# All transpose-bank evictions on VectorE, and the next head's expansion moved ahead of the last iteration's matmuls, in an eight-core latent-attention kernel

## The chip, the cores and the metric

The kernel runs on the eight cores of one Trainium2 chip. Its time is device microseconds of the slowest core, from a run of the whole program. Each core computes the same steps on its own rows of the input; there is no exchange between cores.

## The reference

One layer of latent attention and a gated low-rank feed-forward part, each followed by a residual and a layer norm. Batch 2, sequence 4096, model width 4096, 32 heads. Cut to what matters:

```python
q   = _rmsnorm(x @ wq_a.T, q_a_ln_w) @ wq_b.T            # 32 heads x 128
ckv, k_pe = split(x @ wkv_a.T)                           # 256 latent + 64 rope
kv  = _rmsnorm(ckv, kv_a_ln_w) @ wkv_b.T                 # per head: 64 k_nope + 128 v
# rope on q_pe and k_pe, k_pe shared by all heads
scores = einsum('bqhd,bkhd->bhqk', q_full, k_full) * softmax_scale
attn   = softmax(where(causal, scores, min))
out    = einsum('bhqk,bkhd->bqhd', attn, v) @ wo.T
x = _layernorm(x + out)
# feed-forward: 64 experts of rank 8, top 16 gated by a small router
x = _layernorm(x + ((x @ A_w.T) * gate) @ B_w.T * 2.0)
```

## The kernel before

A core owns 1024 of the 8192 query rows: eight tiles of 128, spread so that each core has the same causal work. The stages run one after the other with a barrier between them: the latent keys of all 4096 positions; the query's first and second projection; the attention loop over 32 heads; the output projection with layer norm; the router; the feed-forward part and the last layer norm. Activations lie transposed on chip.

Every instruction is recorded by the helper class `Em` and replayed by `_replay`, whose line 267 emits them all. So each row of the profile says L267, and instructions are told apart by their tiles. Orders and waits are written out by hand: `em.op(engine, ...)` appends to an engine's queue, `em.mark(engine)` gives a token, `em.wait(engine, token)` makes that engine's queue stop until the token is there. Each engine runs its queue strictly in the order in which `em` recorded it.

The attention loop stands in lines 799 to 890. An iteration is one head, one slot (a tile of 128 queries; eight slots, `NSLOT`) and one block of 1024 keys. Slots need 1, 2, 3, 4, 1, 2, 3, 4 blocks (`TRIPS`, line 27), so a head has 20 iterations and the loop has 640. Iteration `r` of the loop records, in this order:

- ScalarE: the exponential of the scores of `r`, from bank `sA` or `sB` (by the parity of r) into `P_sb`. It waits for QK of `r` and the transposes of `r-2`.
- TensorE: QK of `r+1` (two matmuls of 512 columns into the other score bank), which needs the exponential of `r-1` to have left that bank.
- TensorE: PV of `r-1` (eight matmuls into `mix` or `mix2`), which waits for the eviction of `r-1`.
- TensorE: eight transposes of `P_sb` into `ptP`, which wait for the exponential of `r`. Their token is `tok_pvt[r]`.
- If `r-1` was the last block of its slot, the finish of that slot: VectorE reciprocal and multiply, a TensorE transpose into `mix`, a VectorE copy into the output tile (`fin_done`, `fin_act_prev`).
- The eviction of `ptP` into `PT_sb`, token `tok_evac[r]`: with the causal mask on VectorE if `r` is the last block of its slot; otherwise a plain copy, on VectorE for even `r` and on ScalarE for odd `r` (line 870).

Keys and values of a head are made from the latent ones by `emit_expansion` (line 740), just before the head's first iteration: eight blocks, each with 2 matmuls for the keys, which VectorE casts into `Kf`, and 8 matmuls for the values, which ScalarE casts into `Vx`. All of it goes through one score bank, and each block's key matmuls wait for the cast of the block before, and likewise the value matmuls. `Kf` and `Vx` have two buffers. At a head boundary, that is where `nxt["h"] != cur["h"]`, the QK of the next iteration is not recorded in its usual place: the expansion and that QK stand at the end of the iteration (lines 882 to 886), behind PV, the transposes and the eviction.

Of the kernel before, what the change touches and what calls it, by code (L numbers as in the profile page):

```python
# [294 lines left out]
def build(debug=False, race_detect=True, upto="F"):  # L295
# [56 lines left out]
    with ExitStack() as ctx:  # L352
        em = Em(nc, ctx)
        _LAST_EM[0] = em
        _emit(nc, em, d, ctx, debug, upto)
        _replay(nc, em, ctx)
# [3 lines left out]
def _emit(nc, em, d, ctx, debug, upto="F"):  # L360
# [332 lines left out]
    with ExitStack() as pctx:  # L693
# [9 lines left out]
        scores = [sA, sB]  # L703
# [17 lines left out]
        for h in range(H):  # L721
            for s in range(NSLOT):
                for kb in range(TRIPS[s]):
                    if s == 0 and kb == 0:
                        first_it[h] = len(iters)
                    iters.append(dict(h=h, s=s, kb=kb, first=(kb == 0),
                                      last=(kb == TRIPS[s] - 1)))
# [3 lines left out]
        tok_exp = [None] * N  # L731
# [8 lines left out]
        def emit_expansion(h, bank):  # L740
            hp = h % 2
            war = tok_flash_done.get(h - 2)
            ev = []
            kn_ev = [None] * 8
            v_ev = [None] * 8
            em.waits("pe", [t_wkvb])
            for b in range(8):
                if b >= 1:
                    em.wait("pe", kn_ev[b - 1])
                for c in range(2):  # L750
                    em.opw("pe", [t_wkvb], "matmul", bank[0:64, 0:512],
                           wkvb_sb[c][:, h * 192: h * 192 + 64],
                           cnorm[c][:, b * 512:(b + 1) * 512],
                           start=(c == 0), stop=(c == 1))
                t_kn = em.mark("pe")
                em.waits("dve", [t_kn, war, t_init, t_init_p])
                em.op("dve", "tensor_copy", Kf[hp][0:64, b * 512:(b + 1) * 512],
                      bank[0:64, 0:512])
                kn_ev[b] = em.mark("dve")
                ev.append(kn_ev[b])  # L760
                if b >= 1:
                    em.wait("pe", v_ev[b - 1])
                for sub in range(4):
                    kk = b * 4 + sub
                    for c in range(2):
                        em.opw("pe", [t_wkvb], "matmul",
                               bank[:, 512 + sub * 128: 512 + sub * 128 + 128],
                               cnorm[c][:, kk * 128:(kk + 1) * 128],
                               wkvb_sb[c][:, h * 192 + 64: h * 192 + 192],
                               start=(c == 0), stop=(c == 1))  # L770
                t_v = em.mark("pe")
                em.waits("act", [t_v, war, t_init, t_init_p])
                dst = Vx[hp][:, b * 4 * VSTRIDE:(b + 1) * 4 * VSTRIDE]
                dst = dst.rearrange("p (s w) -> p s w", w=VSTRIDE)[:, :, 0:128]
                em.op("act", "copy", dst,
                      bank[:, 512:1024].rearrange("p (s w) -> p s w", w=128))
                v_ev[b] = em.mark("act")
                ev.append(v_ev[b])
            tok_exp_ready[h] = ev

        def emit_qk(it):
            cu = iters[it]
            par = it % 2
            hp = cu["h"] % 2
            if it - 2 >= 0:
                em.wait("pe", tok_exp[it - 2])
            em.waits("pe", tok_exp_ready.get(cu["h"], []))
            kb = cu["kb"]
            lhsQ = Q[:, cu["h"] * 1024 + cu["s"] * 128: cu["h"] * 1024 + cu["s"] * 128 + 128]
            for hh in range(2):  # L790
                em.op("pe", "matmul", scores[par][:, hh * 512:(hh + 1) * 512],
                      lhsQ, Kf[hp][:, kb * 1024 + hh * 512: kb * 1024 + hh * 512 + 512],
                      start=True, stop=True)
            tok_qk[it] = em.mark("pe")
# [4 lines left out]
        for r in range(N + 1):  # L799
            prev = iters[r - 1] if r >= 1 else None  # L800
            cur = iters[r] if r < N else None
            nxt = iters[r + 1] if r + 1 < N else None

            if cur is not None:
                par = r % 2
                em.wait("act", tok_qk[r])
                if r - 2 >= 0:
                    em.wait("act", tok_pvt[r - 2])
                em.op("act", "activation", P_sb[par][:], scores[par][:], AF.Exp,
                      scale=SCALE)  # L810
                tok_exp[r] = em.mark("act")

            boundary = (nxt is not None and cur is not None
                        and nxt["h"] != cur["h"])
            if nxt is not None and not boundary:
                emit_qk(r + 1)

            if prev is not None:
                parp = (r - 1) % 2
                sp = prev["s"] % 2  # L820
                em.wait("pe", tok_evac[r - 1])
                if prev["first"] and fin_done[sp] is not None:
                    em.wait("pe", fin_done[sp])
                em.waits("pe", [fin_act_prev[0]])
                hpp = prev["h"] % 2
                kbp = prev["kb"]
                for t in range(8):
                    em.opw("pe", [tok_evac[r - 1]], "matmul", pv_[sp],
                           PT_sb[parp][:, t * 128:(t + 1) * 128],
                           Vx[hpp][:, (kbp * 8 + t) * VSTRIDE:  # L830
                                     (kbp * 8 + t) * VSTRIDE + 129],
                           start=(prev["first"] and t == 0),
                           stop=(prev["last"] and t == 7))

            if cur is not None:
                em.wait("pe", tok_exp[r])
                if r - 2 >= 0:
                    em.wait("pe", tok_evac[r - 2])
                for t in range(8):
                    em.opw("pe", [tok_exp[r]], "transpose",  # L840
                           ptP[par][:, t * 128:(t + 1) * 128],
                           P_sb[par][:, t * 128:(t + 1) * 128], idn16[:])
            tok_pvt[r] = em.mark("pe")

            if prev is not None and prev["last"]:
                sp = prev["s"] % 2
                h_, sf = prev["h"], prev["s"]
                em.wait("dve", tok_pvt[r])
                if fin_pe_prev[0] is not None:
                    em.wait("dve", fin_pe_prev[0])  # L850
                em.op("dve", "reciprocal", rcp_c, pv_[sp][:, 128:129])
                em.self_edge("dve")
                em.op("dve", "tensor_tensor", att_tm, pv_[sp][:, 0:128],
                      rcp_c.broadcast_to((128, 128)), op=ALU.mult)
                t_fin = em.mark("dve")
                fin_done[sp] = t_fin
                em.waits("pe", [t_fin, fin_act_prev[0]])
                em.opw("pe", [t_fin], "transpose", atp, att_tm, idn16[:])
                t_atp = em.mark("pe")
                fin_pe_prev[0] = t_atp  # L860
                em.wait("dve", t_atp)
                em.op("dve", "tensor_copy",
                      Q[:, h_ * 1024 + sf * 128: h_ * 1024 + sf * 128 + 128],
                      atp)
                fin_act_prev[0] = em.mark("dve")
                if sf == NSLOT - 1:
                    tok_flash_done[h_] = fin_act_prev[0]

            if cur is not None:
                e = "dve" if (cur["last"] or r % 2 == 0) else "act"  # L870
                em.wait(e, tok_pvt[r])
                if cur["last"]:
                    fam = 0 if cur["s"] < 4 else 1
                    em.op(e, "tensor_tensor", PT_sb[par][:], ptP[par][:],
                          mask2[:, fam * 1024:(fam + 1) * 1024], op=ALU.mult)
                elif e == "act":
                    em.op(e, "copy", PT_sb[par][:], ptP[par][:])
                else:
                    em.op(e, "tensor_copy", PT_sb[par][:], ptP[par][:])
                tok_evac[r] = em.mark(e)  # L880

            if boundary:
                if r - 1 >= 0:
                    em.wait("pe", tok_exp[r - 1])
                emit_expansion(nxt["h"], scores[(r + 1) % 2])
                emit_qk(r + 1)

        em.barrier()
        if debug:
# [408 lines left out]
```

How the kernel before makes its waits and increments, by code:

```python
        def body(h):  # L264
            for entry in em.stream[e]:
                meth, args, kw, sem, n = entry[:5]
                ins = getattr(h, meth)(*args, **kw)
                for s, v in (entry[5] if len(entry) > 5 else ()):
                    ins._wait_ge(s, v)
                if sem is not None:
                    ins.then_inc(sem, n)
```

## Time and profile before

| | us |
|---|---|
| time, median of 3 runs | 4692.8 |
| time, lowest and highest | 4672.8 and 4705.76 |
| the profiled execution | 4672.8 |
| its span on the slowest core (core 5) | 4671.3 |
| spans of all eight cores | 4646.4 to 4671.3 |
| TensorE busy, share of the span | 2900.7, 62% |
| ScalarE busy | 1229.8, 26% |
| VectorE busy | 1019.7, 22% |
| GpSimd busy | 355.2, 8% |

In rows of the order of time, the columns are start (us from the span's start), duration (us), engine, line, operation, output<-input, shape, count; a bracket gives the idle time of the engine just before and what ended it. PE is TensorE, PEld its weight loads, DVE VectorE, ACT ScalarE; "PEq" and the like are an engine's sequencer, from which a semaphore came, and "issue" is idle time for which the profile shows no wait. A row "x8" is eight instructions back to back, with their total.

### The profile page before, as it was taken

The numbers are of one execution on the slowest core, as the hardware profiler recorded it, in microseconds if no ns is written. First come the engines' busy times: TensorE is split into PE (matmuls) and PEld (weight loads), VectorE is DVE, ScalarE is ACT, GpSimd is POOL, SyncE is SP. The second block draws the span as 40 slices with busy tenths as digits, with TensorE's granted clock in tenths as the row PEclk, the third lists the DMA queues.
The fourth block names the chain that finished last, engine by engine and source line by source line (L and its number), as shares of the span: only waits on it lengthen the run. The fifth ranks groups of instructions, "written<-read, shape, count | busy, mean of one in ns | idle before, by whom it ended". The sixth has DMA issues, their size and how long they took to land.

```text
span 4671.3 us, 53309 instructions; the slowest of 8 cores (4646.4 to 4671.3 us)
## 1 busy us (share of the span) xinstructions
PE 2900.7 (62%) x19214; PEld 1416.4 (30%) x19214; DVE 1019.7 (22%) x1923; ACT 1229.8 (26%) x1280; POOL 355.2 (8%) x466
## 2 busy tenths in 40 slices
PE   2771734444666666666676666666668888827650
PEld 0220311111333334333344333333333333302110
DVE  0110000001222222222222222222220000062116
ACT  0000001111444444444444444444430000000110
POOL 4431002322000000000000000000010000000000
PEclk9886977776989999999978999999999999957775
DMA  8867140002000000000000000000033333210003
GB/s 120 117 90 121 24 72 0 0 0 45 1 1 1 1 1 1 1 1 1 1 1 1 1 1 1 1 1 1 1 57 85 81 82 82 67 37 0 0 0 144
DMA packets 76490, 145.64 MB, mean 31 GB/s; under 512 B 12306, under 2 KB 53396, under 8 KB 70228
## 3 DMA queue, kind: packets, MB, share of 16 engines
q0 software_dynamic: 67792, 116.29, 14.9%
q1 hardware_dynamic: 8452, 25.95, 1.5%
q8 instruction: 169, 2.77, 0.2%
q14 instruction: 77, 0.63, 0.0%
HBM read 233.31 MB, written 16.78 MB: 54 GB/s over the span
## 4 chain that ended last, share of the span: by engine, by line
PEldq 32%; issue 18%; PEld 16%; DVE 14%; ACT 7%; DMA 4%; POOL 2%; DVEq 2%; POOLq 2%; ACTq 1%; another core or an unknown queue 1%; SPq 0%
PEldq L267 32%; DVE AR L267 14%; ACT AR L267 7%; PEld mix L267 4%; PEld psE L267 3%; PEld sA L267 3%; POOL AR L267 2%; DVEq L267 2%; POOLq L267 2%; PEld psL L267 1%; ACTq L267 1%; PEld ptP L267 1%; DMA AR<-xT 1%; DMA AR<-wqbT 1%
## 5 line engine op out<-in xcount | busy, mean ns | idle before, releaser
L267 PE MATMUL sA<-AR 128*128 128x128 bf16 (+2 forms) x3200 | 546.5, 296 | 186.7 <-issue 55.9
L267 PE MATMUL mix<-AR 128*128 128x129 bf16 x5120 | 425.2, 229 | 276.5 <-DVEq L267 189.5
L267 PEld LDWEIGHTS mix<-AR 128*128 128x128 bf16 x5120 | 323.0, 101 | 588.4 <-DVEq L267 387.3
L267 PE MATMUL psE<-AR 128*128 128x512 bf16 x2048 | 479.7, 398 | 14.9 <-issue 10.5
L267 PE MATMUL ptP<-idn,AR 128*128 128x128 bf16 x5120 | 422.2, 230 | 37.5 <-ACTq L267 37.5
L267 ACT ACTIVATE AR<-sB,consts 128x1024 bf16<-128x1024 f32 x320 | 356.3, 1113 | 128.4 <-PEq L267 95.9
L267 ACT ACTIVATE AR<-sA,consts 128x1024 bf16<-128x1024 f32 x320 | 356.2, 1113 | 89.4 <-PEq L267 69.2
L267 ACT COPY AR<-ptP 128x1024 bf16<-128x1024 bf16 x192 | 194.3, 1012 | 648.2 <-PEq L267 648.2
L267 PEld LDWEIGHTS ptP<-idn,AR 128*128 128x128 bf16 x5120 | 340.1, 103 | 52.3 <-ACTq L267 48.3
L267 ACT ACTIVATE AR<-AR 128x1024 bf16<-128x1024 bf16 (+3 forms) x76 | 76.4, 1006 | 1042.9 <-DVEq L267 1042.9
L267 PEld LDWEIGHTS sA<-AR 128*128 128x128 bf16 (+1 forms) x3200 | 205.6, 104 | 417.3 <-issue 394.4
L267 PEld LDWEIGHTS psE<-AR 128*128 128x128 bf16 x2048 | 205.6, 101 | 289.8 <-issue 74.2
L267 ACT CAST AR<-sA 128x512 bf16<-128x512 f32 x256 | 149.8, 585 | 417.7 <-PEq L267 408.8
L267 DVE TENSOR_TENSOR AR<-ptP,AR 128x1024 bf16<-128x1024 bf16 x256 | 177.1, 692 | 361.3 <-PEq L267 353.3
L267 PE MATMUL psL<-AR 128*128 128x512 bf16 (+1 forms) x768 | 186.2, 408 | 89.7 <-DMA AR<-xT 82.8
L267 DVE CAST AR<-sA 64x512 bf16<-64x512 f32 x256 | 174.8, 683 | 273.8 <-PEq L267 272.0
L267 PE MATMUL sB<-AR 128*128 128x512 bf16 x640 | 208.3, 410 | 25.7
L267 DVE COPY AR<-ptP 128x1024 bf16<-128x1024 bf16 x192 | 132.8, 692 | 418.6 <-PEq L267 410.8
L267 PE MATMUL psC<-AR 128*128 128x512 bf16 x512 | 176.0, 520 | 65.5 <-DMA AR<-wqbT 58.6
L267 PE MATMUL mix<-idn,AR 128*128 128x128 bf16 x256 | 56.3, 220 | 246.5 <-DVEq L267 246.5
L267 POOL DMA_DIRECT2D AR<-A_sta x32 | 16.9, 664 | 2317.3 <-DVEq L267 2317.3
L267 PE MATMUL psB<-AR 128*128 128x512 bf16 x512 | 114.5, 386 | 103.2 <-DMA AR<-wqaT 103.2
(91 smaller groups left out, 1734.1 us busy)
## 6 DMA issues: line engine op xcount, KB each, us to landing
AR<-xT POOLq DMA_DIRECT2D x256, 128.0 KB, 9.6
AR<-wo_sta POOLq DMA_DIRECT2D x32, 1024.0 KB, 9.6
AR<-xoT SPq DMA_DIRECT2D x32, 512.0 KB, 9.1
AR<-xoT POOLq DMA_DIRECT2D x32, 256.0 KB, 20.2
AR<-wqaT POOLq DMA_DIRECT2D x4, 2048.0 KB, 65.6
AR<-wqbT POOLq DMA_DIRECT2D x8, 1024.0 KB, 28.0
out<-AR SPq DMA_DIRECT2D x16, 512.0 KB, 2.7
out<-AR POOLq DMA_DIRECT2D x16, 512.0 KB, 2.9
```

What stands on the lines that cost most here:

```text
L267: ins = getattr(h, meth)(*args, **kw)
```

## The change

Two edits in the attention loop. First, the expansion of the next head and the QK of its first iteration no longer stand at the end of the last iteration of a head, but in QK's usual place: ahead of PV of the iteration before and of the last iteration's own transposes. The wait of TensorE for the exponential that frees the score bank moves with them. Second, the eviction of `ptP` is always on VectorE.

```diff
@@ -810,9 +810,11 @@
                       scale=SCALE)
                 tok_exp[r] = em.mark("act")
 
-            boundary = (nxt is not None and cur is not None
-                        and nxt["h"] != cur["h"])
-            if nxt is not None and not boundary:
+            if nxt is not None:
+                if cur is not None and nxt["h"] != cur["h"]:
+                    if r - 1 >= 0:
+                        em.wait("pe", tok_exp[r - 1])
+                    emit_expansion(nxt["h"], scores[(r + 1) % 2])
                 emit_qk(r + 1)
 
             if prev is not None:
@@ -867,7 +869,7 @@
                     tok_flash_done[h_] = fin_act_prev[0]
 
             if cur is not None:
-                e = "dve" if (cur["last"] or r % 2 == 0) else "act"
+                e = "dve"
                 em.wait(e, tok_pvt[r])
                 if cur["last"]:
                     fam = 0 if cur["s"] < 4 else 1
@@ -878,12 +880,6 @@
                 else:
                     em.op(e, "tensor_copy", PT_sb[par][:], ptP[par][:])
                 tok_evac[r] = em.mark(e)
-
-            if boundary:
-                if r - 1 >= 0:
-                    em.wait("pe", tok_exp[r - 1])
-                emit_expansion(nxt["h"], scores[(r + 1) % 2])
-                emit_qk(r + 1)
 
         em.barrier()
         if debug:
```

## Rows read from the trace of the kernel before

**Rows 1.** Spans and mean granted TensorE clock of the cores: the slowest.
```profile
core 5: 4671.3 us, clock 0.858
```

**Rows 2.** The attention loop's stretch: busy us (instructions) per engine, clock, DMA share, GB/s.
```profile
1154.00:3470.00 2316.00, 1563.25 (x14319) 906.38 (x14316) 658.78 (x1470) 1055.98 (x1087) 1.50 (x3) 0.93 0.01 2
```

**Rows 3.** Order of time, one head: T9, its eviction, T10.
```profile
2132.04 0.61 PE L267 MATMUL ptP<-idn,AR 128*128 128x128 bf16 x8
2132.78 0.69 DVE L267 TENSOR_TENSOR AR<-ptP,AR 128x1024 bf16<-128x1024 bf16 x1 [1.37 <-PEq L267]
...
2134.11 0.61 PE L267 MATMUL ptP<-idn,AR 128*128 128x128 bf16 x8
```

**Rows 4.** The same, from T10 to T11: VectorE evicts behind a finish.
```profile
2136.35 0.69 DVE L267 TENSOR_TENSOR AR<-ptP,AR 128x1024 bf16<-128x1024 bf16 x1
...
2137.22 0.62 PE L267 MATMUL mix<-AR 128*128 128x129 bf16 x8 [0.65 <-DVEq L267]
2137.68 0.61 PE L267 MATMUL ptP<-idn,AR 128*128 128x128 bf16 x8
```

**Rows 5.** The same, from T11 to T12: ScalarE evicts beside a finish.
```profile
2138.40 1.01 ACT L267 COPY AR<-ptP 128x1024 bf16<-128x1024 bf16 x1 [3.83 <-PEq L267]
...
2140.47 0.62 PE L267 MATMUL mix<-AR 128*128 128x129 bf16 x8 [0.34 <-issue]
2140.93 0.61 PE L267 MATMUL ptP<-idn,AR 128*128 128x128 bf16 x8
```

**Rows 6.** The same, from T17 to T18: ScalarE evicts, nothing is finished.
```profile
2153.95 0.61 PE L267 MATMUL ptP<-idn,AR 128*128 128x128 bf16 x8
...
2154.67 1.01 ACT L267 COPY AR<-ptP 128x1024 bf16<-128x1024 bf16 x1 [3.83 <-PEq L267]
2155.78 1.11 ACT L267 ACTIVATE AR<-sA,consts 128x1024 bf16<-128x1024 f32 x1
...
2157.06 0.61 PE L267 MATMUL ptP<-idn,AR 128*128 128x128 bf16 x8 [0.59 <-ACTq L267]
```

**Rows 7.** Costliest groups: the plain evictions; busy us, mean ns, idle before and releaser.
```profile
L267 ACT COPY AR<-ptP 128x1024 bf16<-128x1024 bf16 x192 | 194.3, 1012 | 648.2 <-PEq L267 648.2
...
L267 DVE COPY AR<-ptP 128x1024 bf16<-128x1024 bf16 x192 | 132.8, 692 | 418.6 <-PEq L267 410.8
```

**Rows 8.** Order of time at a head boundary: T18, PV, T19, QK, PV, T0.
```profile
2016.64 0.61 PE L267 MATMUL ptP<-idn,AR 128*128 128x128 bf16 x8 [0.59 <-ACTq L267]
...
2018.24 0.62 PE L267 MATMUL mix<-AR 128*128 128x129 bf16 x8 [0.99 <-DVEq L267]
...
2018.70 0.61 PE L267 MATMUL ptP<-idn,AR 128*128 128x128 bf16 x8
...
2033.49 0.59 PE L267 MATMUL sA<-AR 128*128 128x512 bf16 x2 [0.86 <-ACTq L267]
...
2034.85 0.63 PE L267 MATMUL mix<-AR 128*128 128x129 bf16 x8
2035.48 0.61 PE L267 MATMUL ptP<-idn,AR 128*128 128x128 bf16 x8
```

**Rows 9.** Slow transposes: first and last stretched T2 of the 27 heads, one T19.
```profile
1399.96 1.06 PE L267 MATMUL ptP<-idn,AR 128*128 128x128 bf16 x8
...
3276.74 1.06 PE L267 MATMUL ptP<-idn,AR 128*128 128x128 bf16 x8
...
2159.28 1.06 PE L267 MATMUL ptP<-idn,AR 128*128 128x128 bf16 x8
```

**Rows 10.** Stretches of one head each, 27 in a row: first, best, worst, sum and mean.
```profile
1368.40:1448.20 79.80, 56.81 (x450) 32.00 (x451) 20.67 (x47) 33.02 (x34) 0.00 (x0) 0.78 0.00 1
...
2091.50:2161.60 70.10, 46.17 (x449) 26.76 (x447) 20.64 (x46) 33.02 (x34) 0.00 (x0) 0.98 0.00 1
...
2375.60:2458.70 83.10, 60.67 (x450) 34.34 (x451) 20.67 (x47) 33.02 (x34) 0.00 (x0) 0.73 0.00 1
...
sum 1956.00, PE 1324.78 PEld 769.16 DVE 556.99 ACT 891.48 POOL 0.00; mean PE 49.07 PEld 28.49 DVE 20.63 ACT 33.02 POOL 0.00
```

## The prediction, made before the changed kernel was run

> **What bounds the kernel now.** I read the span of the slowest core first. It is 4671.3 us [rows 1], and the profiled execution took 4672.8, so 1.5 us lie around the span. Its time is the lowest of three: the median is 4692.8. Every difference below is worked out in the profiled execution, then taken off the median.
>
> Then I cut the span by stage. The attention loop is the stretch from 1154 to 3470, 2316 us [rows 2]. TensorE is busy 1563 us of it, ScalarE 1056, VectorE 659: nobody is full, so the loop goes by a chain of hand-overs, and busy shares cannot price the change. The change touches nothing outside this stretch.
>
> So I read the order of time inside one head and measured from the start of one transpose group to the next. I call the group of iteration i of a head T0 to T19, and the step to it by the two numbers. There are four kinds of step, and apart from the clock (below) they repeat to 0.02 us:
>
> - *VectorE evicts, nothing else.* T9 at 2132.04, its eviction of 0.69 us at 2132.78, T10 at 2134.11: 2.07 us [rows 3].
> - *VectorE evicts and a slot is finished in between.* The eviction starts only at 2136.35, behind reciprocal, multiply and copy, and PV waits for it ("0.65 <-DVEq"): T10 to T11 is 3.57 us [rows 3, 4].
> - *ScalarE evicts, a slot is finished.* The copy of 1.01 us runs beside VectorE's finish. PV is released by none of the two: T11 to T12 is 3.25 us [rows 4, 5].
> - *ScalarE evicts, nothing finished.* The copy of 1.01 us starts at 2154.67 and the exponential queued behind it at 2155.78. T18 waits for that exponential ("0.59 <-ACTq"), and comes 3.11 us after T17 [rows 6].
>
> **The evictions, one by one.** A head has 20 iterations. Its 8 last ones of a slot are evicted by VectorE anyway, with the mask. Of the other 12, the 6 with odd r go to ScalarE today: iterations 1, 3, 11, 13 (each finishing the slot before) and 7, 17 (plain). That gives 6 x 32 = 192, which is the count of the ScalarE copies [rows 7]. ScalarE's queue loses 192 x 1.012 = 194 us, VectorE's gains 192 x 0.692 = 133 [rows 7]. Neither figure is the gain, since both lie under other work. The price is the kind of step that each becomes:
>
> - 4 x 32 steps go from 3.25 to 3.57: +0.32 each, **+41.0 us**. This is a loss: the eviction, today beside the finish, is queued behind it.
> - 2 x 32 steps go from 3.11 to 2.06: -1.05 each, **-67.2 us**. What is late next there is PV's usual wait for VectorE, which is inside the 2.06.
>
> No other queue moves: ScalarE's exponential no longer has a copy ahead of it, and VectorE at 659 + 133 = 792 us of 2316 is 34% busy.
>
> The Trainium skill speaks against this half of the change: "Use both ScalarE and VectorE for PSUM evacuation" (TensorEngine Tiling (Array Packing), section PSUM Bottleneck). By that rule alone the sum would stop at the first item, a loss; the trace agrees with it on the 128 steps with a finish and not on the 64 without.
>
> **The head boundary.** Today iteration 19's PV waits 0.99 us for the eviction of 18, with no QK to fill the time; then come T19, the expansion of the next head (16 groups into one score bank), two QK, PV, T0. T18 is at 2016.64, T19 at 2018.70, the first QK at 2033.49, T0 at 2035.48: 18.84 us from T18 to T0 [rows 8]. In the new order the expansion stands right behind T18. It needs only the exponential of 18, which T18 already waited for, and the expansion's first VectorE cast stands behind one eviction, as today. So:
>
> - T18 to the first QK: 14.79 us, what T19 to the first QK takes today (2033.49 - 2018.70).
> - first QK, then PV of 18 and T19, both free to run. Today two QK groups take 1.36 us up to PV at 2034.85, 0.68 each, and PV takes 0.63 up to T0 [rows 8]: 0.68 + 0.63 = 1.31 us.
> - T19 to T0: a plain VectorE step with QK inside, 2.06 us.
>
> That makes 18.16, or -0.68 at each of 31 boundaries: **-21 us**. The wait of 0.99 is hidden by the expansion, and the wait for the masked eviction of 19, which the expansion hides today, comes out, but with a QK inside. The finish of slot 7 stays behind T0. The bounds: if QK's place fills nothing, the gain is 0; if the whole 0.99 goes, -31 us. I take -21, by the steps above.
>
> Sum of the hand-overs: 41.0 - 67.2 - 21 = **-47 us**.
>
> **The clock.** The granted clock changes between its two levels, 1.2 and 2.4 GHz, and the rows show it twice over: the whole loop's mean is 0.93 [rows 2], and eight transposes that take 0.61 us take 1.06 [rows 9]. Undisturbed, the steps of a head add up to 68.8 us: 9 steps of 2.06, 4 of 3.57, 4 of 3.25, 2 of 3.11, and 16.78 from T19 to T0 [rows 3 to 6, 8]. The 27 heads from 1368 to 3324 take 72.4 on the mean, 70.1 at best (clock 0.98) and 83.1 at worst (0.73) [rows 10]. So the low clock costs some 3.65 us a head, over twice what the hand-overs of a head promise. I went through all 27 for where it stands:
>
> - T1 to T2 is stretched in 23 of 27, T2 to T3 with it, by 0.8 each on the mean (first and last such T2 [rows 9]): 1.4 us a head. It comes after two thin steps, T0 to T1 (3.57) and the one after.
> - T11 to T12 in 10 of 27, T12 to T13 with it: 0.4 us a head.
> - T19 and the first blocks of the expansion in 19 of 27, after T17 to T18 (3.11, ScalarE's copy) and the 0.99 wait: T19 takes 1.06 [rows 9]. With the expansion's own slow blocks this is about 1.1 to 1.3 us a head, and both worst heads, 79.8 and 83.1 [rows 10], begin with an expansion slow from end to end.
>
> The change takes away both thin places ahead of the third (3.11 becomes 2.06, the bare wait goes): -1.2. It makes four steps thinner (3.57 for 3.25), two of them second in a pair. For T11 to T13 I move the frequency half way to that of T1 (10 to 16.5 of 27, at 1.2): +0.3. T1 to T3 become certain: +0.2. Two single thin steps, priced as T6 to T7 and its follower behave now (0.15 a head): +0.15. Net -0.6 x 32 = **-19 us**; its ends are +48 (1.5 a head more) and -72 (2.25 a head fewer).
>
> Sum: -47 - 19 = -66, or 4607 for an execution like the profiled one, and 4692.8 - 66 = **4627** against the median.
>
> The Trainium skill names the danger: where TensorE idles briefly between groups that cycle through PSUM, its clock gate falls and rises again (TensorE: Matmul & The Clock Gate, A second HAM failure mode). Steps of 3.57 us with a low clock behind them agree with this, and by that rule alone the four thinner steps would cost more than I give them.
>
> **The rivals.**
>
> 1. *The clock gives the gain back* (0.21). The low clock moves with the phase of the heads and falls into every pair of thin steps, and into singles, while the head end stays slow. For it: T1 to T2 in 23 of 27. Against: T16 to T17, a single thin step, is followed by a stretched step in one of 27. -47 + 48: 4693, no change.
> 2. *The clock mostly recovers* (0.17). Without the slow head end, one fall a head is left, costing 1.4: -47 - 72: 4574.
> 3. *Slower: a low clock that holds* (0.08). One mechanism: a fall after T0 to T2 that lasts as in the head at 2375.6, 83.1 us against the mean of 72.4, +10.7 a head [rows 10]. Seven such heads eat the 66 us, eleven make the kernel over 1% slower; fourteen give 4627 + 150 = 4777. Against: both such heads begin at the head end, which gets denser.
> 4. *The freed ScalarE shortens nothing* (0.04). If the plain steps stay at 3.11, because something other than the copy holds them: +41 - 21 = 4713. T9 to T10 at 2.07 speaks against it.
>
> **How the numbers follow.** My forecast has 0.50, alone from 4600 to 4665. A measurement of this kernel tells about 1% from no change, 47 us, so the border is 4646. Faster: 0.17 of rival 2 and 0.42 of my 0.50, 0.59. Slower by over 1%: 0.08. The same: the rest, 0.33. The range from 4570 to 4705 takes in my case, rival 1 and most of rival 2, and leaves out rival 3 and parts of 2 and 4.
>
> **What would show it.** In the new profile: no ScalarE copy out of the transpose bank, 384 VectorE copies; T17 to T18 and T7 to T8 at 2.06; T1 to T2, T3 to T4, T11 to T12, T13 to T14 at 3.57; the expansion right behind T18 and 18.2 us from T18 to T0; T19 with transposes of 0.61; a granted clock in the loop of at least 0.93. I am wrong if a step with a finish comes out over 3.6 at full clock, if PV of 18 waits after the expansion, or if the loop's clock falls below 0.91.

## The result, and the profile after

| | before | after |
|---|---|---|
| median, us | 4679.2 (12 runs) | 4605.0 (12 runs) |
| profiled execution's span, slowest core | 4671.3 | 4599.9 |
| attention loop, first to last key cast, slowest core | 2256.2 | 2179.3 |
| the same, mean of eight cores | 2238.4 | 2166.7 |
| low clock inside it, mean of eight cores | 248 | 218 |

The changed kernel takes 0.9827 of the time before, with a 95% interval of 0.9801 to 0.9854: 81 us less, 67 to 93. The range forecast held it. Of the 22 us between the 4627 forecast and the 4605 measured, 14 are the kernel before: its median was 4692.8 in the three runs on which the forecast was built, and 4679.2 in twelve. The loop accounts for 72 us on the mean of the cores and the rest of the kernel is unchanged in code; I take the loop from its first to its last key cast, since that row is there for every kernel and every core. In some executions, of most of these kernels, the cores of one die ran longer at a lower clock than those of the other; the ratios leave these executions out, and the evictions alone have no ratio below because only one of their four remained. "Low clock" is how long the trace's clock records show 1.2 GHz in that stretch, counted from 30 us after the first key cast: the 30 us before it hold 12 to 28 us at 1.2 GHz (mean of the cores) in every kernel, also in those that show none afterwards.

One row of the changed kernel for [rows 1], one for [rows 2], columns as there:

```profile
core 1: 4599.9 us, clock 0.860
```

```profile
1154.00:3398.60 2244.60, 1533.44 (x14326) 902.97 (x14326) 791.38 (x1663) 864.34 (x896) 4.50 (x9) 0.93 0.01 2
```

ScalarE is down from 1056 to 864 us and VectorE up from 659 to 791, the 194 and 133 of the prediction. The mean clock is 0.93 as before. The plain evictions are now one group, from the page's costliest groups (busy, mean ns, idle before), for [rows 7]:

```profile
L267 DVE COPY AR<-ptP 128x1024 bf16<-128x1024 bf16 x384 | 265.5, 691 | 312.8 <-PEq L267 289.2
```

The order of time at a head boundary, for [rows 8]: T18, the expansion's first matmuls, later the first QK, PV, T19, and T0.

```profile
2134.68 0.61 PE L267 MATMUL ptP<-idn,AR 128*128 128x128 bf16 x8
...
2135.36 1.31 PE L267 MATMUL sA<-AR 128*64 128x512 bf16 x10
...
2149.41 0.59 PE L267 MATMUL sA<-AR 128*128 128x512 bf16 x2 [0.86 <-ACTq L267]
...
2150.09 0.63 PE L267 MATMUL mix<-AR 128*128 128x129 bf16 x8
...
2150.56 0.61 PE L267 MATMUL ptP<-idn,AR 128*128 128x128 bf16 x8
...
2152.62 0.61 PE L267 MATMUL ptP<-idn,AR 128*128 128x128 bf16 x8
```

The expansion stands right behind T18 and the wait of 0.99 is gone. T18 to T0 takes 17.94 us, where [rows 8] had 18.84. Inside the head, in the place of [rows 4, 5]: T10, T11 and T12, the second step with the eviction that was ScalarE's.

```profile
2177.20 0.61 PE L267 MATMUL ptP<-idn,AR 128*128 128x128 bf16 x8
...
2179.27 0.61 PE L267 MATMUL ptP<-idn,AR 128*128 128x128 bf16 x8
...
2182.38 0.62 PE L267 MATMUL mix<-AR 128*128 128x129 bf16 x8 [0.65 <-DVEq L267]
...
2182.84 0.61 PE L267 MATMUL ptP<-idn,AR 128*128 128x128 bf16 x8
```

2177.20 and 2179.27 are T9 and T10, 2.07 apart; T11 follows 3.57 later, with PV released by VectorE. T12 comes after another 3.57 in that head, for 3.25 before. Over the 30 heads measured, every step has the length forecast when the clock is up: eleven of 2.06 from T19 on, eight of 3.57, 15.86 us from T18 to T19. A head adds up to 67.0 us, and the best one measured comes within 0.4 of it (for [rows 10]; the best here, a common one, a bad one):

```profile
1365.60:1433.00 67.40, 44.74 (x451) 26.28 (x449) 24.72 (x52) 27.01 (x28) 0.00 (x0) 1.00 0.00 1
1433.00:1501.30 68.30, 46.07 (x451) 27.02 (x449) 24.75 (x52) 27.01 (x28) 0.00 (x0) 0.98 0.00 1
...
2060.80:2136.30 75.50, 54.13 (x452) 32.21 (x450) 24.74 (x53) 27.01 (x28) 0.00 (x0) 0.82 0.00 1
```

The mean of the 30 heads is 69.9 us, so the low clock still costs 2.8 us a head (3.65 before). It stands elsewhere: at the head end in 2 of 30 heads (19 of 27 before), at T1 to T2 in 19 of 30, at T11 to T12 in 13, and right behind each single step with a finish in 4 to 11. The count for T1 to T2 is no accident of the slowest core: it is 17 to 21 of 30 on the eight cores, and 20 to 24 in the kernel before.

Two theories were to be told apart. *Hand-overs*: each edit is worth its steps, and the clock adds what the dense head end spares. *Clock*: the gain is mostly a different amount of low clock, and says little about the edits.

### The profile page after: what moved, and what is told of

The parts are those of the page before. It is cut to its first block, busy times and chain, and to the rows that moved or that the text cites. A ratio compares the mean times of both kernels' runs of the same rounds, so it can differ in the third digit from the quotient of the medians.

```text
span 4599.9 us, 53214 instructions; the slowest of 8 cores (4561.5 to 4599.9 us)
## 1 busy us (share of the span) xinstructions
PE 2868.7 (62%) x19214; PEld 1411.7 (31%) x19214; DVE 1151.5 (25%) x2115; ACT 1037.7 (23%) x1088; POOL 355.2 (8%) x466
## 4 chain that ended last, share of the span: by engine, by line
PEldq 32%; DVE 18%; issue 17%; PEld 15%; DMA 5%; ACT 3%; DVEq 3%; POOL 2%; POOLq 2%; ACTq 1%; another core or an unknown queue 1%; SPq 0%
PEldq L267 32%; DVE AR L267 18%; PEld mix L267 4%; PEld psE L267 3%; ACT AR L267 3%; DVEq L267 3%; PEld sA L267 3%; POOL AR L267 2%; POOLq L267 2%; PEld psL L267 1%; ACTq L267 1%; DMA AR<-wqbT 1%; DMA AR<-xT 1%; DMA out<-AR 1%
## 5 line engine op out<-in xcount | busy, mean ns | idle before, releaser
L267 PE MATMUL sA<-AR 128*128 128x128 bf16 (+2 forms) x3200 | 519.2, 284 | 190.2 <-DVEq L267 58.5
L267 DVE COPY AR<-ptP 128x1024 bf16<-128x1024 bf16 x384 | 265.5, 691 | 312.8 <-PEq L267 289.2
L267 PEld LDWEIGHTS sA<-AR 128*128 128x128 bf16 (+1 forms) x3200 | 193.9, 100 | 403.7 <-issue 380.9
L267 DVE TENSOR_TENSOR AR<-psE,AR 128x1024 bf16<-128x1024 f32 x32 | 39.2, 1225 | 579.5 <-PEq L267 579.5
```

What stands on the lines that cost most here:

```text
L267: ins = getattr(h, meth)(*args, **kw)
```

## The experiments

The loop's time and its low clock, means of the eight cores of one profiled execution each, and the sum of the undisturbed steps of a head:

| kernel | steps of a head | loop | low clock | ratio to before (interval) |
|---|---|---|---|---|
| before | 68.8 | 2238 | 248 | 1 |
| changed | 67.0 | 2167 | 218 | 0.983 (0.980 to 0.985) |
| boundary only | 67.9 | 2158 | 73 | 0.982 (0.977 to 0.987) |
| evictions only | 67.9 | 2168 | 104 | none |
| ScalarE beside a finish | 65.3 | 2113 | 204 | 0.981 (0.973 to 0.990) |
| changed, fillers | 67.0 | 2107 | 1 | 0.972 (0.963 to 0.981) |
| before, fillers | 68.7 | 2173 | 46 | 0.981 (0.971 to 0.991) |
| boundary only, fillers | 67.9 | 2133 | 0 | 0.975 (0.964 to 0.985) |
| ScalarE beside a finish, fillers | 65.3 | 2052 | 0 | 0.957 (0.942 to 0.972) |
| finish deferred | 58.1 | 1828 | 0 | 0.910 (0.899 to 0.921) |
| finish two later | 59.2 | 1861 | 4 | 0.916 (0.913 to 0.920) |
| eight small copies | 67.1 | 2180 | 254 | 0.986 (0.981 to 0.991) |
| four small copies | 67.1 | 2174 | 226 | 0.983 (0.979 to 0.988) |
| longer on TensorE | 67.7 | 2158 | 106 | 0.981 (0.976 to 0.985) |

### Each edit alone

Boundary only: the changed kernel with the old choice of engine.

```diff
-                e = "dve"
+                e = "dve" if (cur["last"] or r % 2 == 0) else "act"
```

> Only the new order at the head boundary; the evictions alternate between VectorE and ScalarE as before. If the two edits add up by their hand-overs, this is worth 18.84 - 17.93 = 0.91 us at each of 31 boundaries (both measured in the two traces), 28 us: 4651 against 4679 for the kernel before, with the steps inside a head unchanged (3.25, 3.11). If the clock's share of the gain comes with the bare wait at the head end, another 10 to 20 us go: 4635. The rival, that all of the gain comes from the faster engine for the evictions: 4679.

Measured: 4598.2 us, 80 less than the kernel before beside it. That is below both expected values (4651 and 4635), and it is the whole gain of the change. The steps are as expected: T19 to T0 2.06, the ScalarE steps 3.25 and 3.11, T18 to T0 0.9 us shorter than before. What was not expected is the low clock, 73 us in place of 248. From the order of time of the slowest core, T1 to T2 is stretched in 6 of 30 heads, which before it was in 23 of 27, though these two steps are the same instructions; on the eight cores it is 3 to 8 of 30. The loop's stretch in this kernel's trace, for [rows 2]:

```profile
1165.00:3395.00 2230.00, 1483.32 (x14329) 862.67 (x14330) 658.99 (x1471) 1058.46 (x1088) 5.05 (x10) 0.97 0.01 3
```

Evictions only: the kernel before with line 870 reading `e = "dve"`.

> Only the evictions, all on VectorE; the head boundary as before. By the hand-overs: 128 steps from 3.25 to 3.57, 64 from 3.11 to 2.06, +41 - 67 = -26 us: 4653. If the clock's share comes with the density of T17 to T18, 10 to 20 us more: 4638. The rival, that the eviction's own duration counts (1.01 to 0.69 us, 192 times, 61 us): 4618, with the steps that hold a finish no longer than 3.25.

The profiled execution took 4605.2 us. One execution is too few for a ratio, so the time by itself decides little. The trace does: T18 to T19 and the start of the expansion are undisturbed although the bare wait is still there, the four steps with a finish are 3.57, the plain ones 2.06. So it is not the eviction's own duration that counts: the steps with a finish got longer, as the hand-overs have it, although their eviction got 0.32 us shorter. The low clock is 104 us here, and T1 to T2 is stretched in 2 to 5 of 30 heads on the eight cores, although its steps are the 3.57 of the changed kernel.

So either edit alone lowers the low clock to 73 or 104 us, and both together bring it back to 218. This does not rest on three traces alone: the granted clock of the whole span (mean of the eight cores) is 0.863 to 0.865 in the eight executions of the changed kernel that the ratio uses, 0.879 to 0.882 in the three of the boundary alone, and 0.876 in the one of the evictions alone. By loop and by time, moving the evictions on top of the new boundary is worth nothing: 2158 becomes 2167, and 4598 becomes 4605.

### The clock held up

In four kernels I put eight matmuls of the identity, read by nobody, into the wait ahead of each finish's transpose.

```diff
+                em.waits("pe", [fin_act_prev[0]])
+                for _ in range(8):
+                    em.op("pe", "matmul", (mix, mix2)[1 - sp][:, 192:320],
+                          idn16[:], idn16[:], start=True, stop=True)
                 em.waits("pe", [t_fin, fin_act_prev[0]])
```

> The changed kernel with eight extra 128-column matmuls of the identity, whose result nobody reads, in TensorE's wait ahead of each finish's transpose (0.95 us wide). They compute nothing of the result. If the low clock comes from the thin steps with a finish, it goes: a head takes 67 to 68 us instead of the 69.9 measured, the loop's granted clock is over 0.97, and the kernel 4605 - 75 = 4530. If the low clock has nothing to do with these steps, the time stays at 4605 or rises by what of the fillers sticks out of the wait, up to 256 x 0.1 = 25 us.

Measured: 4536.8 us, 68 less than the changed kernel (by the two ratios, 50 less). Seven of the eight cores show no low clock in the loop, one shows 7 us. One row of the loop's stretch:

```profile
1154.00:3330.00 2176.00, 1601.49 (x16387) 961.60 (x16388) 792.14 (x1664) 862.66 (x896) 7.04 (x14) 0.99 0.01 3
```

TensorE does more (1601 us busy for 1533), and the loop is 72 us shorter on this core (2107 for 2179). The eight cores' loops lie within 3 us (2106 to 2109), where those of the changed kernel lie within 27. Work that nobody needs, put into a wait, makes the kernel faster: the low clock goes when the waits in the thin steps with a finish are filled, and it cost the changed kernel some 60 us.

> The kernel before, with the same eight extra matmuls ahead of each finish's transpose; they compute nothing of the result. It takes the clock out of the comparison: if the hand-overs of the change are worth 1.74 us a head (68.8 to 67.0), the attention loop from its first to its last key cast is 31 x 1.74 = 54 us longer than the 2107 of the changed kernel with fillers, 2161, and the kernel 4537 + 54 = 4591. If the low clock at the head end stays, because the fillers don't stand there, some 20 to 30 us more: 4615. If the gain of the change was mainly the clock, the two kernels with fillers differ by under 20 us: 4550.

> Only the new head boundary, evictions alternating as before, and the fillers (nothing of the result). Without fillers this edit alone took all of the gain. If the evictions on VectorE are worth their hand-overs (26 us) and a low clock has eaten them, then with the clock held up they show again: the loop is 26 us longer than 2107, 2133, and the kernel 4563. If moving the evictions is worth nothing in itself, loop and kernel equal those of the changed kernel with fillers: 2107 and 4537.

Measured: 4601.7 us for the kernel before and 4575.3 for the boundary alone. With the clock up, the loops can be laid side by side (first and last key cast, the slowest core's row of each: before, boundary only, changed, all with fillers):

```profile
L267 DVE CAST AR<-sA x256: 681/682/684, 1144.0 to 3329.4; 64x512 bf16<-64x512 f32 x128
```

```profile
L267 DVE CAST AR<-sA x256: 682/683/684, 1156.4 to 3284.7; 64x512 bf16<-64x512 f32 x128
```

```profile
L267 DVE CAST AR<-sA x256: 682/683/684, 1155.9 to 3263.1; 64x512 bf16<-64x512 f32 x128
```

On the mean of the eight cores they are 2173, 2133 and 2107 us. Moving the evictions is worth 25 us, where the steps say 26: that term stands, once the clock can't eat it. The boundary is worth 40, of which the steps say 28. The other 12 us go with the 46 us of low clock that the fillers didn't remove from the kernel before: they don't stand at the head end, where T19 and the first blocks are still stretched (T18 to T19 in 8 of 30 heads). That is the place which the new boundary makes dense. The size fits: in the four kernels that ran with fillers and without, the loop lost 25 to 65 us for 73 to 217 us less low clock, 0.27 to 0.34 us for each, and 12 for 46 is 0.26.

The change's hand-overs are then 1.74 x 31 = 54 us of the loop's 72, and the remaining 18 us are clock.

### Which engine should evict

The changed kernel, with ScalarE in the six iterations of a head that finish a slot and need no mask.

```diff
-                e = "dve"
+                e = "act" if (cur["first"] and not cur["last"]) else "dve"
```

> The changed kernel, but the plain eviction goes to ScalarE in exactly those iterations in which a slot is finished and no mask is needed (6 a head); everything else stays on VectorE. If the hand-over decides: 192 steps from 3.57 to 3.25, -61 us against 4605: 4544, and with fewer falls of the clock down to 4515. If the faster engine is what counts: 192 x 0.32 us lost, 4605 to 4666.

> The changed kernel with ScalarE evicting beside a finish (6 a head), and the fillers (nothing of the result). Without fillers the loop's shortest heads were 1.5 us shorter and the mean was 2113 instead of 2167 us, with wide spread between cores. With the clock held up: 2107 - 6 x 31 x 0.32 = 2048, the same on all cores, and the kernel 4478. If the fillers stick out of TensorE's wait, which ends earlier on this path: 2048 to 2080.

Without fillers: 4602.7 us, the same as the changed kernel within the intervals. By its time the rival would be right; by its trace it isn't: the steps are 3.25 to 3.4 as the hand-overs say, and the loop's mean is 53 us shorter, but it spreads from 2087 to 2150 us over the cores, and the slowest one sets the time. T1 to T2 is stretched in 26 of 30 heads of the slowest core. With fillers the loop is 2052 us (expected 2048), 55 less than the changed kernel with the same fillers, and within 8 us on all cores. The two executions behind its ratio took 4468.5 and 4503.9 us; the ratio of 0.957 (0.942 to 0.972) to 4679 gives 4478, the expected value, but the interval is wide and the loop says more. So where VectorE has a finish to do, ScalarE is the better engine for the eviction though it takes 1.01 us for 0.69: the Trainium skill's "Use both ScalarE and VectorE for PSUM evacuation" (TensorEngine Tiling (Array Packing), section PSUM Bottleneck) holds here, on those steps, by some 0.3 us each (3.25 to 3.29 for 3.57), and fails on the plain steps, where ScalarE's exponential waits behind its copy.

### The finish off the path

The finish costs 1.5 us in each of eight steps of a head, 12 us a head, where the hand-overs of this change bring 1.74. Here it is recorded behind the eviction, and its transpose and copy one iteration later, into the bank of the slot that is finished.

```diff
-            if prev is not None and prev["last"]:      # ahead of the eviction
...
-                em.waits("pe", [t_fin, fin_act_prev[0]])
-                em.opw("pe", [t_fin], "transpose", atp, att_tm, idn16[:])
...
                 tok_evac[r] = em.mark(e)
+
+            if pend[0] is not None:                    # finished one iteration ago
+                spf, h_, sf, t_fin = pend[0]
...
+                em.opw("pe", [t_fin], "transpose", atps[spf], att_tm, idn16[:])
...
+            if prev is not None and prev["last"]:      # reciprocal and multiply
...
+                pend[0] = (sp, prev["h"], prev["s"], em.mark("dve"))
```

(Shortened, with notes of mine behind `#`; `...` stands for lines left out.)

> The changed kernel with the finish of a slot moved behind the eviction on VectorE and its transpose and copy one iteration later, so that neither PV nor QK waits for it; the transpose goes into the bank of the slot that is finished. The whole result is computed. If the finish sits on the path of a step, as its 3.57 against 2.06 says, all steps take 2.06 and a head 67.0 - 8 x 1.5 = 55 us: the loop 1717 instead of 2167, the kernel 4155, with hardly any low clock outside the expansion. The rival: VectorE or TensorE then holds the step, by 0.2 to 0.5 us (the finish is 0.88 us of VectorE's time and 0.22 of TensorE's): a head 57 to 59, the kernel 4215 to 4280.

Measured: 4253.2 us, a ratio of 0.910 (0.899 to 0.921), the fastest kernel of the study. It lies within what was expected if VectorE or TensorE then holds the step (4215 to 4280, a head of 57 to 59 us), and 98 above the value for steps of 2.06. The loop is 1828 us, within 7 on all cores, without low clock. Against the changed kernel with fillers it is 279 us shorter, and the steps say 8.9 x 31 = 276; the other 59 of the 338 us against the changed kernel itself are the low clock. Steps with a finish take 2.42, two of them 2.53, not 2.06. First one of the two, then a step of 2.42, each from one T to the next:

```profile
2118.38 0.61 PE L267 MATMUL ptP<-idn,AR 128*128 128x128 bf16 x8
...
2119.11 0.69 DVE L267 COPY AR<-ptP 128x1024 bf16<-128x1024 bf16 x1 [0.60 <-PEq L267]
...
2119.21 0.22 PE L267 MATMUL mix<-idn,AR 128*128 128x128 bf16 x1 [0.23 <-issue]
...
2119.51 0.60 PE L267 MATMUL sB<-AR 128*128 128x512 bf16 x2
2119.99 0.22 DVE L267 COPY AR<-mix 128x128 bf16<-128x128 bf16 x1 [0.19 <-issue]
...
2120.45 0.62 PE L267 MATMUL mix<-AR 128*128 128x129 bf16 x8 [0.34 <-DVEq L267]
...
2120.91 0.61 PE L267 MATMUL ptP<-idn,AR 128*128 128x128 bf16 x8
...
2121.64 0.69 DVE L267 TENSOR_TENSOR AR<-ptP,AR 128x1024 bf16<-128x1024 bf16 x1 [0.66 <-PEq L267]
...
2121.74 0.22 PE L267 MATMUL mix<-idn,AR 128*128 128x128 bf16 x1 [0.23 <-issue]
...
2122.04 0.60 PE L267 MATMUL sA<-AR 128*128 128x512 bf16 x2
...
2122.87 0.62 PE L267 MATMUL mix<-AR 128*128 128x129 bf16 x8 [0.23 <-DVEq L267]
...
2123.33 0.61 PE L267 MATMUL ptP<-idn,AR 128*128 128x128 bf16 x8
```

In both, VectorE's eviction is over (2119.80 and 2122.33) before QK is (2120.11 and 2122.64): the finish's transpose stands ahead of QK and pushed it back. In the step of 2.42, PV starts 0.23 behind QK. In the longer one it is the first PV of a slot and must also wait for the finish's copy out of its bank, which ends at 2120.21. TensorE's order thus holds six of the eight steps, so I tried to put that transpose behind QK, in PV's wait, one iteration later still.

```diff
+            while pend and (pend[0][5] <= r - 2 or r == N):   # ahead of PV, behind QK
+                spf, h_, sf, t_fin, at_, _ = pend.pop(0)
+                ...
```

> The kernel with the deferred finish (4253 us), where a step with a finish still takes 2.42 to 2.53 us because the finish's transpose stands between two QK groups' places on TensorE. Here that transpose comes behind QK two iterations later, in TensorE's wait for the eviction. The whole result is computed. If TensorE's order sets these steps: 2.06 to 2.15 us, a head 55 to 56.5 instead of 58.4, the loop 31 x 2 to 3 = 60 to 95 us shorter than 1828, the kernel 4160 to 4190. If VectorE holds them: no change, 4240 to 4260.

Measured: 4292.8 us, 40 slower than the one before; both expected values missed. Single steps with a finish are still 2.42, and where two finishes follow each other one step takes 3.23. In the order of time:

```profile
2083.26 0.22 PE L267 MATMUL mix<-idn,AR 128*128 128x128 bf16 x1 [0.23 <-DVEq L267]
...
2084.12 0.22 DVE L267 COPY AR<-mix 128x128 bf16<-128x128 bf16 x1 [0.19 <-issue]
...
2084.52 0.62 PE L267 MATMUL mix<-AR 128*128 128x129 bf16 x8 [1.04 <-DVEq L267]
```

PV waits 1.04 us behind that transpose for VectorE: the next slot's PV goes into the bank out of which the finish is still copied, and the copy stands in VectorE's queue behind the next finish's reciprocal and multiply, until 2084.34. What holds the single steps at 2.42 there I leave open; the transpose had its wait of 0.23 and PV another 0.23 after it, "issue", which the profile doesn't explain further.

### Does the low clock hang on the length of a head?

The boundary edit has 73 us of low clock and the changed kernel 218, with heads of 67.9 and 67.0 us of steps. To tell length from thinness I wanted the changed kernel's steps in a longer head.

```diff
                 em.waits("dve", [t_kn, war, t_init, t_init_p])
+                if True:
+                    em.op("dve", "tensor_copy", dbg_it_sb[:, 0:1], consts[:, 0:1])
```

That is eight copies an expansion; the second kernel has `if b % 2 == 1` there, four copies.

> The changed kernel with one small VectorE copy (one column, read by nobody, nothing of the result) ahead of each of the eight key casts of an expansion: the head gets longer by eight times 0.06 to 0.15 us, its steps stay as they are. The changed kernel has 218 us of low clock in the loop (mean of the cores), the boundary edit alone 73, though most of its steps are the same; its heads are 0.85 us longer. If the low clock hangs on how long a head is, that is on where its thin steps come to lie, it changes strongly here, to under 150 us, and the loop gets no longer than 2167 + 20 - 25 = 2162, or even shorter, in spite of the added work. If it hangs on how thin the steps are, it stays at 200 to 240 us and the loop is 2167 + 15 to 37 us: 2182 to 2204, the kernel 4620 to 4642.

> The same small copy in every second block only: the head gets longer by half as much. If the low clock hangs on the thinness of the steps: loop 2175 to 2186, low clock 200 to 240 us. If it hangs on the length of a head, a third value of the low clock, between that of the changed kernel and that of the run with eight copies or outside both; the loop then doesn't follow the added work (10 to 18 us).

Measured: 4625.7 and 4608.5 us, low clock 254 and 226 us. But the experiment missed its aim: a head's steps add up to 67.1 us in both, as without the copies. One of them takes 0.15 us and disappears in the slack between a key cast and the matmul that waits for it:

```profile
2100.91 0.15 DVE L267 COPY AR<-consts 128x1 f32<-128x1 f32 x1 [0.91 <-PEq L267]
2100.98 0.67 DVE L267 CAST AR<-sA 64x512 bf16<-64x512 f32 x1
```

So they decide nothing about the length. They serve as two repeats: heads of 67.0 us had 218, 254 and 226 us of low clock. (In the second, the four cores of one die also show 0.81 of the clock for 68 to 131 us of the loop, a third value beside 1 and 0.5; it is not counted as low clock. It goes with the longer loops of that die, 2172 to 2193 us for 2159 to 2174.) The next one puts the added work on TensorE, whose own order sets the expansion's pace.

```diff
                     em.wait("pe", v_ev[b - 1])
+                for _ in range(1 + b % 2):
+                    em.opw("pe", [t_wkvb], "matmul", bank[:, 512:640],
+                           cnorm[0][:, b * 512:b * 512 + 128],
+                           wkvb_sb[0][:, h * 192 + 64: h * 192 + 192],
+                           start=True, stop=True)
```

> The changed kernel with twelve extra 128-column matmuls in each expansion (one or two a block, overwritten by the real ones, nothing of the result), this time on the engine whose own order sets the expansion's pace: the head should get longer by 12 x 0.06 to 0.08 = 0.7 to 1.0 us, to about the 67.9 us of the boundary edit alone; the steps between T19 and T18 stay as in the changed kernel. If the low clock hangs on the length of a head, it falls from the 218 to 279 us of the three runs with 67.0 us heads towards the 73 us of the boundary edit alone, and the loop is 2167 + 26 - 50 = 2143, shorter in spite of more work. If it hangs on the thin steps with a finish, which are the same, it stays at 200 to 280 us and the loop is 2167 + 26 = 2193 or more, the kernel over 4625.

Measured: 4601.2 us, against an expected 4625 or more if thinness alone decided. A head's steps add up to 67.7 us, 0.6 more (0.85 aimed at). The loop is not 19 us longer but 9 us shorter than that of the changed kernel, with 106 us of low clock on the mean (68 to 126 on the single cores). T1 to T2, the same instructions with the same thin steps, is stretched in 2 to 4 of 30 heads on the eight cores, for 17 to 21. The granted clock of the whole span is 0.875 to 0.878 in its four executions, for 0.863 to 0.865. So where the low clock falls and how much of it there is does not follow from how thin the steps with a finish are. The mean of 9 us is within what two executions of one kernel differ by; the low clock and the stretched T2 are not. Two cores of this execution, too, ran part of the loop at 0.81 (140 and 143 us, not counted as low clock); one row of core 0:

```profile
1495.00:1556.00 61.00, 44.09 (x393) 25.69 (x393) 20.64 (x42) 22.82 (x25) 0.00 (x0) 0.81 0.00 1
```

That the length of a head is what decides is not shown. For it: among the kernels without fillers and with the finish in its place, the five with heads of 65.3, 67.0 or 68.8 us have 204 to 254 us of low clock, and the three with 67.7 to 67.9 have 73 to 106, among them the evictions alone, with the changed kernel's thin steps and no added work. Against it: these kernels differ at the head end as well, and the twelve matmuls here also fill waits in the expansion, right ahead of T1. Why one head is better than another I didn't settle.

## Why the prediction was right, point by point

- **Evictions, +41.0 and -67.2 us.** Right. Steps with a finish are 3.57 and plain ones 2.06; with the clock held up the edit is worth 25 us against 26.
- **Boundary, -21 us.** Right in kind, short by 7. T18 to the first QK is 14.73 (14.79 said). From the first QK to T19 it is 1.15 us, not 1.31: I had taken 0.63 for PV up to the transposes from [rows 8], where T0 was held by its exponential; freed of it, PV takes 0.47. That is 17.94 for 18.16, 0.90 a boundary, 28 us.
- **Hand-overs together, -47 us.** 54 measured.
- **The clock, -19 us.** The number came out (18), most of its terms didn't. The head end became dense, as said: stretched in 2 of 30 heads. "T1 to T3 become certain" was wrong, 19 of 30; T11 to T12 came to 13 of 30, where half way to T1 would have been 18. Single steps with a finish, which I had priced at 0.15 us for two, are followed by a stretched step in 4 to 11 of 30 heads, and the bad heads of 75 us start at T1 to T2. I had counted places of one trace and carried the counts over to heads of another length; the boundary edit alone, the evictions alone and the twelve matmuls in the expansion show that such counts don't carry over. So this term was right by luck: the same reckoning gives the boundary edit alone at most the head end's 1.2 x 32 = 38 us, and it got 80 - 28 = 52.
- **The sum.** -66 said, -81 measured (67 to 93): 7 us are the boundary, the rest is within the interval. Since the clock's 18 us came by luck, so did that part of the agreement; the hand-overs, 47 of the 66, were right within 7.
- **The rivals.** "The clock gives the gain back" did not happen to the change as a whole, but it is what happens to its second edit: 25 us in steps, and nothing left of them in the kernel. "The freed ScalarE shortens nothing" fell with the plain steps at 2.06. No low clock held on as in the slower rival, though heads of 75 us are 5 of the 30.
- **The signs named.** All came, but for one: the mean clock stayed at 0.93, as the prediction had as its least.

## What to carry to other kernels

Price a change of engine or order by the step from one hand-over to the next, once per kind of step: the same move of an eviction cost 0.32 us beside a finish and gained 1.05 us without one, while the eviction's own duration fell in both. Before judging an edit of some 1% on a TensorE that waits a lot, compare the two kernels with the waits filled by matmuls that nobody reads: here that took the spread between cores from 27 us to 3 and showed the two edits at 40 us (28 of them steps, 12 a low clock that the fillers had left) and 25 us, when their plain runs said 80 and nothing. And look at what the step waits for longest before tuning around it: putting the finish off the path took the changed kernel from 4605 to 4253 us, another 352 us or 7.6%, over four times the change itself.

## What the runs showed of the hardware that I had not expected

- Matmuls that compute nothing made the kernel 1.5% faster by the medians (4605.0 to 4536.8; 1.1% by the ratios), by keeping the granted clock at 2.4 GHz: 218 us of low clock became 1. The Trainium skill's warning that the clock gate falls and rises where TensorE idles briefly between groups (TensorE: Matmul & The Clock Gate, A second HAM failure mode) agrees with this.
- The amount of low clock is not additive over edits: 248 us before, 73 and 104 with one edit each, 218 with both, although each edit shortens the head. Adding 0.6 us of matmuls to each head took 218 to 106.
- In two executions some cores ran part of the loop at a granted clock of 0.81, a value between the two others, for 68 to 143 us.
- A small VectorE copy of one column takes 0.15 us, and eight of them a head left its steps at 67.1 us.
